# A delta-rule layer with a ternary feed-forward: weights of the output projection and the first o and A fetched in the recurrence's last cycle

## What is computed

```python
        def _delta_rule(q, k, v, a, beta):
...
            def step(St, inp):
                q_t, k_t, v_t, a_t, b_t = inp
                err = jnp.einsum('bhvk,bhk->bhv', St, k_t) - v_t
                St = a_t[..., None] * St - (b_t[..., None] * err)[..., None] * k_t[:, :, None, :]
                o_t = jnp.einsum('bhvk,bhk->bhv', St, q_t)
                return (St, o_t)
...
        o = _delta_rule(q, k, v, a, beta)
        mu = jnp.mean(o, axis=-1, keepdims=True)
        var = jnp.mean(jnp.square(o - mu), axis=-1, keepdims=True)
        o = (o - mu) * lax.rsqrt(var + 1e-05) * ln_w + ln_b
        g = jax.nn.sigmoid(x @ Wg).reshape(b, s, NH, DV)
        o = (o * g).reshape(b, s, NH * DV)
        return o @ Wo
...
        up = jnp.einsum('bsd,ed->bse', x, wu)
        gate = jnp.einsum('bsd,ed->bse', x, wg)
        hidden = jax.nn.silu(up) * gate
        return jnp.einsum('bse,de->bsd', hidden, wd)
...
    x = _layernorm(x + _L0_attn_ref(x, ...), axis=-1)
    x = _layernorm(x + _L0_ffn_ref(x, L0_ffn_W_up, L0_ffn_W_gate, L0_ffn_W_down), axis=-1)
```

## Time and profile before

| | us |
|---|---|
| median of 3 runs | 2807.29 (2800.23 to 2809.53) |
| the profiled execution | 2809.65 |
| its span, first to last instruction | 2807.9 |
| TensorE busy in it | 2580.0 |
| VectorE, GpSimd, ScalarE busy | 2031.4, 1435.8, 1204.8 |
| mean granted TensorE clock | 0.964 |

### The profile page before, as it was taken

How to read it: one execution, slowest core, us unless ns; L and a number is a source line. 1 busy time by engine, 2 the same in 40 slices (tenths; PEclk the granted TensorE clock), 3 DMA queues, 4 the chain that set the end, 5 groups by cost and what they waited for, 6 DMA issues and landing times. The chain is left out here.

```text
span 2807.9 us, 50612 instructions
## 1 busy us (share of the span) xinstructions
PE 2580.0 (92%) x17812; PEld 2217.5 (79%) x17922; DVE 2031.4 (72%) x5887; ACT 1204.8 (43%) x2393; POOL 1435.8 (51%) x1215
## 2 busy tenths in 40 slices
PE   8999999999999499999999999999639997899999
PEld 6888878887888388888888888888527776788887
DVE  4776777677768279899999999999548885433333
ACT  4455445545544233333333333334458774433333
POOL 2644543454355488999899898888222220000000
PEclk9999999999999799999999999999659998999999
DMA  5466455645654855555656665556364553100000
GB/s 132 128 176 190 143 146 168 180 142 153 174 166 123 281 187 211 197 197 207 226 225 228 223 232 208 196 206 227 123 262 164 198 206 108 80 12 11 11 11 15
DMA packets 417320, 454.39 MB, mean 162 GB/s; under 512 B 122496, under 2 KB 367232, under 8 KB 393856
## 3 DMA queue, kind: packets, MB, share of 16 engines
q1 hardware_dynamic: 417152, 452.22, 48.5%
HBM read 321.49 MB, written 131.14 MB: 161 GB/s over the span
## 5 line engine op out<-in xcount | busy, mean ns | idle before, releaser
L355 PE MATMUL pa_ps<-pa_x_hi,pa_w_hi 128*128 128x512 f32 x1296 | 507.3, 391 | 11.0 <-ACT pa_y L298 6.8
L355 PE MATMUL pa_ps<-pa_x_lo,pa_w_hi 128*128 128x512 f32 x1296 | 505.1, 390 | 0.0
L355 PE MATMUL pa_ps<-pa_x_hi,pa_w_lo 128*128 128x512 f32 x1296 | 504.9, 390 | 0.0
L438 DVE SCALAR_TENSOR_TENSOR pa_cv<-pa_y,pa_taps,pa_cv 128x2048 f32<-128x2048 f32 x144 | 354.6, 2462 | 17.8
L1182 DVE TENSOR_TENSOR pb_tmp<-pb_gb,pb_ps 128x112 f32<-128x112 f32 (+6 forms) x1792 | 331.0, 224 | 23.2 <-POOL pb_gb L774 9.3
L774 POOL TENSOR_TENSOR pb_gb<-pb_gb,pb_ng 128x448 f32<-128x448 f32 (+6 forms) x448 | 331.7, 787 | 4.2 <-DMA pb_gb<-scratch_pairs 4.2
L1187 DVE TENSOR_TENSOR pb_ps<-pb_ps,pb_tmp 128x112 f32<-128x112 f32 (+6 forms) x1792 | 332.6, 228 | 0.0
L355 PEld LDWEIGHTS pa_ps<-pa_x_hi,pa_w_hi 128*128 128x128 f32 x1296 | 243.5, 188 | 69.2 <-ACT pa_y L298 11.5
L758 POOL TENSOR_TENSOR pb_UT<-pb_UT,pb_crow 128x1024 f32<-128x1024 f32 x120 | 281.9, 2368 | 5.8 <-DMA pb_crow<-scratch_crow 5.8
L355 PEld LDWEIGHTS pa_ps<-pa_x_hi,pa_w_lo 128*128 128x128 f32 x1296 | 243.7, 188 | 51.1
L355 PEld LDWEIGHTS pa_ps<-pa_x_lo,pa_w_hi 128*128 128x128 f32 x1296 | 243.7, 188 | 50.0
(11 more groups left out here) (193 smaller groups left out, 5421.5 us busy)
## 6 DMA issues: line engine op xcount, KB each, us to landing
pb_crow<-scratch_crow SPq DMA_DIRECT2D x30, 2048.0 KB, 9.6
pb_gb<-scratch_pairs SPq DMA_DIRECT2D x64, 896.0 KB, 6.6
pa_o_ng<-scratch_beta SPq DMA_DIRECT2D x16, 1024.0 KB, 7.9
scratch_ng<-pa_o_ng SPq DMA_DIRECT2D x16, 1024.0 KB, 4.5
scratch_A<-pa_o_A SPq DMA_DIRECT2D x16, 1024.0 KB, 4.5
scratch_vt<-pa_o_vt SPq DMA_DIRECT2D x16, 1024.0 KB, 4.5
scratch_q<-pa_o_q SPq DMA_DIRECT2D x16, 1024.0 KB, 6.9
scratch_g<-pa_o_g SPq DMA_DIRECT2D x16, 1024.0 KB, 8.1
```

The costliest lines, as they stand in the source:

```text
L355: last = nc.tensor.matmul(out, w[:, mat, k, :], xx[:, k, b * S:(b + 1) * S], start=(k == 0 and n == 0), stop=(k == KT - 1 and n == 2))
L438: nc.vector.scalar_tensor_tensor(out=out, in0=yy[:, :, k:k + S], scalar=tap(k), in1=out, op0=ALU.mult, op1=ALU.add).then_inc(s_tap, 1)
```

## The change

- `res`, the tile for the stage's results (32 KB of a partition), and a pair of tiles `first` for o and A now exist during the recurrence. UT lies in `res`, KT in `first[0]`, vt in `first[1]`.
- In the recurrence's last cycle SyncE loads, when their readers are done, o of chunk 0 into KT's place, Wo into UT's, and A of chunk 0 into vt's. Behind its last step of that stage GpSimd multiplies the two. SyncE's final wait has the weights' four loads in it.
- `attention_out` finds the product of chunk 0 and the weights in place. Its buffers for A and g are its own, and SyncE starts with o and A of chunk 1.
- ScalarE and VectorE wait at their heads for nothing of the columns; the first affine step does.
- The 16 splits of the weights go in three groups of 8, 4 and 4 between the steps of chunk 0, and `low` of chunk 0 stands ahead of the normalisation of chunk 1.

```diff
-        vt = m.sb("vt", [P, HB, CH])
+        vt = first[1][:, :, :].rearrange("p g (i t) -> p (g i) t", t=CH)
...
-        KTr = m.sb("KT", [P, GR, P])
+        KTr = first[0]
...
-        UT = m.sb("UT", [P, HB, P])
+        UT = res[:, :, :].rearrange("p c (g v) -> p (c g) v", v=P)
...
                 if kind == LAST:
-                    feed_forward_weights(4, 8)
+                    feed_forward_weights(4, 6)
+                    sp.wait_ge(s_dp, at_d + D_STATE[3] + 4)
+                    sp.wait_ge(s_os[0], 16)
+                    load(first[0][:, :, :], "o", 0, s_early[0])
+                    feed_forward_weights(6, 8)
+                    sp.wait_ge(s_dp, at_d + D_S[7] + 1)
+                    for j in range(4):
+                        sp.dma_start(res[:, 4 * j:4 * j + 4, :], wo.rearrange("(h p) d -> p h d", p=P)[:, 4 * j:4 * j + 4, :]).then_inc(s_early[1], 16)
+                    feed_forward_weights(8, 9)
+                    sp.wait_ge(s_wv, 2 * c + 2)
+                    sp.wait_ge(s_w, 2 * c + 2)
+                    load(first[1][:, :, :], "A", 0, s_early[0])
                     store_o(c - 1, 1 - p, at_d)
-                    feed_forward_weights(8, PIECES)
+                    feed_forward_weights(9, PIECES)
                     return
...
+            sp.wait_ge(s_early[1], 64)
...
+            pool.wait_ge(s_early[0], 32)
+            tt(first[0][:, :, :], first[0][:, :, :], first[1][:, :, :], ALU.mult).then_inc(s_early[0], 1)
...
-            load(o_in[0], "o", 0, s_o[0])
-            load(a_in[0], "A", 0, s_a[0])
+            load(o_in[1], "o", 1, s_o[1])
+            load(a_in[1], "A", 1, s_a[1])
             sp.dma_start(lnw[:, :], ln_w.rearrange("(p o) -> p o", o=1)).then_inc(s_c, 16)
             sp.dma_start(lnb[:, :], ln_b.rearrange("(p o) -> p o", o=1)).then_inc(s_c, 16)
-            for j in range(4):
-                sp.dma_start(wo_in[j], wo.rearrange("(h p) d -> p h d", p=P)[:, 4 * j:4 * j + 4, :]).then_inc(s_wl[j], 16)
-            load(o_in[1], "o", 1, s_o[1])
+            load(g_in[0], "g", 0, s_g[0])
+            load(a_in[0], "A", 2, s_a[0])
+            load(g_in[1], "g", 1, s_g[1])
+            sp.wait_ge(s_t, 4)
+            load(o_in[0], "o", 2, s_o[0])
             load_x(0, 0)
             load_x(1, 1)
-            sp.wait_ge(s_oa, 1)
-            load(a_in[0], "A", 2, s_a[0])
-            sp.wait_ge(s_t, 4)
-            load(o_in[0], "o", 2, s_o[0])
-            sp.wait_ge(s_wo, 8)
-            load(g_in[0], "g", 0, s_g[0])
-            sp.wait_ge(s_wo, 12)
-            load(a_in[1], "A", 1, s_a[1])
-            sp.wait_ge(s_wo, 16)
-            load(g_in[1], "g", 1, s_g[1])
+            sp.wait_ge(s_oa, 2)
+            load(a_in[1], "A", 3, s_a[1])
             sp.wait_ge(s_t, 8)
             load(o_in[1], "o", 3, s_o[1])
             sp.wait_ge(s_gm, 4)
             load(g_in[0], "g", 2, s_g[0])
-            sp.wait_ge(s_oa, 2)
-            load(a_in[1], "A", 3, s_a[1])
             sp.wait_ge(s_oa, 3)
             load(a_in[0], "A", 4, s_a[0])
...
-            nc.gpsimd.memset(eps[:, :], EPS).then_inc(s_c, 1)
-            for j, (sem, start) in enumerate([(s_p, 2), (s_r, 2), (s_res, 2)]):
+            nc.gpsimd.memset(eps[:, :], EPS).then_inc(s_id, 1)
+            for j, (sem, start) in enumerate([(s_p, 2), (s_r, 2), (s_res, 2), (s_oa, 1)]):
...
-            scaled(0, 0, 0)
+                pool.wait_ge(s_o[p], 16 * i + 16 * p)
+                pool.wait_ge(s_a[p], 16 * i + 16 * p)
+                nc.gpsimd.tensor_tensor(o_in[p][:, :, :], o_in[p][:, :, :], a_in[p][:, :, :], ALU.mult).then_inc(s_oa, 1)
+
             scaled(1, 0, 1)
             scaled(2, 1, 0)
             scaled(3, 1, 1)
...
-            act.wait_ge(s_c, 33)
+            act.wait_ge(s_id, 3)
...
-                if not first:
+                if first:
+                    act.wait_ge(s_c, 32)
+                else:
                     act.wait_ge(s_lo, c - 1)
...
+            def round_weights(first, end):
+                for h in range(first, end):
+                    nc.scalar.activation(wo_hi[:, h, :], res[:, h, :], ACT.Copy).then_inc(s_wh, 1)
+
+            round_weights(0, 8)
             squares(0)
             normal(0)
-            for h in range(NH):
-                if h % 4 == 0:
-                    act.wait_ge(s_wl[h // 4], 16)
-                nc.scalar.activation(wo_hi[:, h, :], wo_in[h // 4][:, h % 4, :], ACT.Copy).then_inc(s_wh, 1)
-            act.wait_ge(s_wo, NH)
+            round_weights(8, 12)
             affine(0, 0, True)
+            round_weights(12, NH)
+            high(0, 0)
             squares(1)
             normal(1)
-            high(0, 0)
             affine(1, 1, True)
...
-            dve.wait_ge(s_c, 33)
...
+            def rest_of_weights(first, end):
+                for h in range(first, end):
+                    dve.wait_ge(s_wh, h + 1)
+                    nc.vector.tensor_tensor(wo_lo[:, h, :], res[:, h, :], fp32(wo_hi[:, h, :]), ALU.subtract).then_inc(s_wo, 1)
+
             means(0)
+            rest_of_weights(0, 8)
             normal(0, True)
-            for h in range(NH):
-                dve.wait_ge(s_wh, h + 1)
-                nc.vector.tensor_tensor(wo_lo[:, h, :], wo_in[h // 4][:, h % 4, :], fp32(wo_hi[:, h, :]), ALU.subtract).then_inc(s_wo, 1)
+            rest_of_weights(8, 12)
+            gate(0, 0, 0)
+            rest_of_weights(12, NH)
             means(1)
-            gate(0, 0, 0)
+            low(0, 0)
             normal(1)
-            low(0, 0)
...
-        recurrence(nc, scr, [W_up, W_gate, W_down], part)
         res = m.sb("res", [P, NCH, HID])
         stat = m.sb("stat", [P, NCH, 2])
-        attention_out(nc, x, Wo, ln_w, ln_b, scr, res, stat)
+        with ExitStack() as inner:
+            first = [Mem(nc, inner, "first").sb(n, [P, NH, CT]) for n in ("o", "A")]
+            recurrence(nc, scr, [W_up, W_gate, W_down], Wo, part, res, first)
+            attention_out(nc, x, ln_w, ln_b, scr, res, stat, first[0])
```

22 lines of the change are left out of this document (7 added, 15 removed).

## The result

The changed kernel takes 2788.86 us (median of 6 runs, 2784.39 to 2792.46), the kernel before beside it 2807.08 (2800.23 to 2813.46). The ratio is 0.9934, with a 95% interval of 0.9916 to 0.9951: 18.5 us less, from 13.8 to 23.6. The forecast was 2790.1 in a range of 2782 to 2798, so the time, the sign and the size came as foretold. The profiled execution of after has a span of 2790.7 us, where that of before has 2807.9.

The account below looks back on a forecast made before the run. The output projection's first product, at 2101.02, sets the rest. Minus 11.1 (start), minus 8.4 (splits), plus 2.0 and 1.3 (VectorE), minus 1.1 (og_lo) gives about 17.2 us earlier: 2790.1 us, range 2782 to 2798.

Parts of the forecast that it names:

- Start of the block: Head of the output projection: TensorE starts at about 2035.9, 11.1 us earlier; eight weight splits ahead of the squares are free.
- First stall: VectorE, chunk 0: GpSimd's multiplication for chunk 1 stops the weight subtractions; reciprocal at 2049.7 instead of 2047.7, 2.0 us lost.
- Second stall: VectorE, before chunk 1's sums: GpSimd's multiplication for chunk 2 holds the last of four subtractions from 2055.5 to 2060.0.
- then the sums: 2068.1: VectorE, chunk 1: after one subtraction, the gate and four more subtractions, the sums end at 2068.1; squares start at 2068.2.
- Squares to first product: From chunk 1's squares to the first product: the old path in its old order, 15.6 us, from 2068.2 to 2083.8.
- Product 0: First product of the output projection: starts at 2083.8, 17.2 us before 2101.02.
- Rival E: First products on TensorE: granted 1.2 GHz; 128 more matmuls at the low clock make it 0.3% slower, about 2817; chance 0.03.
- The recurrence: Its last cycle: the added loads put piece 8 at about 1992, 2.5 us before ScalarE reads it, cost zero.
- rival C: Recurrence's last cycle: early loads come late, piece 8 behind four weight loads; up to 6 us, gain about 10, 2797; chance 0.11.
- B: VectorE's short instructions keep their turn beside GpSimd: 2.0 and 3.9 us not lost, gain 23, about 2784; chance 0.20.
- D: Loop behind the first product isn't ready: up to 5 us of the gain lost in the first chunks, 2795; chance 0.10.
- F: Block's start doesn't move, because the barrier waits for a load or a multiplication: within 0.3%, 2806; chance 0.04.

Follow-up runs that it names:

- all splits first: The changed kernel with all 16 weight splits between normalisation and affine step of chunk 0, and 16 subtractions ahead of the gate; ratio 0.9952 to the kernel before.
- early weights alone: The changed kernel, but o and A of chunk 0 loaded and multiplied in the projection as before, only Wo early; ratio 0.9971 to the kernel before.
- the columns at the heads: The changed kernel with the layer norm's columns awaited at the heads of ScalarE and VectorE again; ratio 0.9964 to the kernel before.
- GpSimd held back: The changed kernel with three added waits that start GpSimd's multiplications for chunks 1, 2 and 3 later; ratio 0.9918 to the kernel before.

## Why the prediction was right, point by point

- **Start of the block: right.** 0.97 us from the block's first load (1.0 in the sum), 11.1 us gained. The eight splits ahead of the squares are free: the squares start at 5.67 us (5.5), and ScalarE even waits 0.67 us for VectorE in front of them.
- **First stall: right.** The eight subtractions took 9.21 us, the reciprocal is at 14.68 us (14.8). The affine step is at 20.00 (20.2), 17.7 us ahead of before (17.5).
- **Second stall: right.** GpSimd's multiplication for chunk 2 starts at 20.29 us (20.6) and holds the subtractions for 4.3 us. The one that was held is the last of the four ahead of the gate, as I had it (5.02 us for 0.68). With these multiplications held back, that time comes back, and with one more it grows.
- **The step that failed: "then the sums: 2068.1".** I knew that the fourth multiplication (chunk 3's) would come at about 31 us, and asked only whether it would hold og_lo. It held pc_nmu, 0.17 us long, which stands in front of the squares: 2.8 us. The fault was in my reading of what can be held ("the same kind as the weight subtractions, both inputs in SBUF"). The trace of before had the row against it. VectorE's groups from 2035 to 2366 us there show a copy with one input of 128x6 elements, 12 times at 2968 ns and 4 times at 162:

```profile
L1561 DVE COPY pc_bn_all<-pc_bn 128x6 f32 x12 | 35.6, 2968 | 0.0
...
L1561 DVE COPY pc_bn_all<-pc_bn 128x6 f32<-128x6 f32 x4 | 0.7, 162 | 0.0
```

  One of them starts at 2123.51 and ends with GpSimd's multiplication, 2121.93 plus 4.61. The same gap made the expectation miss for the kernel with all splits first, and half of it for early weights alone. The other half there, and the kernel with the columns at the heads, is pc_shift: it has both inputs in SBUF, so my reading covered it, but at 0.17 us I hadn't priced it.
- **Squares to first product: sized a little too long.** 15.6 us in the sum, 14.5 in the trace. Part of it is TensorE: the twelve transposes of chunk 2 took 2.47 us, and 2.82 before.
- **Product 0: its clock was left out of the sum.** I kept its length. It took 1.6 us less, because the clock was already at the higher level: it was granted 1.00 from 2087.0 to 2098.0 us, and 0.52 from 2101.0 to 2104.2 before. Its matmuls follow one another by 0.23 us once the second has begun, where the first seven took 0.44 each. Rival E had the clock on the other side.
- So product 1 is at 50.25 us where 48.9 was foretold: 2.5 late for the squares, 1.1 back behind them; and the 1.6 of product 0 makes the total right, 17.5 for 17.2. That the total hit so well is luck in part: one error of 2.5 us, and two of 1.1 and 1.6 the other way.
- **The recurrence: cost zero, but with less margin than I gave it.** The load of Wo is at 1979.99; ScalarE reads piece 8 at 1996.50, 40.4 us ahead of the block's start as before (1994.51, 40.4 ahead), and its row names no idle time. But the piece, issued at 1982.60, took 13.6 us to land, until 1996.2: 0.3 us early, not 2.5. And ScalarE does wait for the next one, piece 9:

```profile
1996.50 0.61 ACT L859 ACTIVATE pb_kq<-pb_kq 128x512 f32<-128x512 f32 x1
...
2004.75 0.63 ACT L859 ACTIVATE pb_kq<-pb_kq 128x512 f32<-128x512 f32 x1 [2.68 <-DMA pb_kq<-in_W_down]
```

  That wait is in every profile of a kernel in which o, Wo and A all come early (0.3 to 3.4 us) and in none of the others. It costs nothing, because ScalarE's next copy of X, at 2010.53, waits 3.84 us for VectorE: it is 26.4 us ahead of the block's start in both kernels (2008.50 before). Piece 8 was the closer one: the copy of X behind it, at 1998.08, waits 0.26 us for VectorE, so by an estimate from these rows some 0.6 us more (0.3 and 0.26) would have begun to cost time, as in rival C.

  Over all profiles, the block starts between 2027.3 and 2038.9 us. The twelve profiles of kernels with early loads have a mean of 2032.4, the two without 2034.9 and 2029.9, mean 2032.4 as well. This spread, up to 0.4% of the time, is there in kernels that are the same up to this point. It is larger than most effects of this study, and of the size of the scatter that gives a 17 us gain an interval of 10 us. Where it comes from stays open.
- **The rivals.** B (no stalls): refuted; held back by hand, the stalls' end gives 7.0 us. C (late pieces: one is, and the slack takes it), D (loop not ready; the transposes at 2098.20 name no idle time), E (lower clock through the first products) and F (start doesn't move) are refuted by the rows above.

## What to carry to other kernels

When an early stage is moved forward, the chain that was second becomes the one to price: here VectorE between GpSimd's multiplications, where 17.7 us won at the affine step left 15.9 at the first product. Before adding or moving work of GpSimd, list every VectorE instruction beside it, the shortest too, and look in the trace for instructions whose duration is many times their least: a 0.17 us instruction that someone waits for costs as much as a large one. Where GpSimd has slack, a wait that puts it behind VectorE's step is free; three waits of that kind gave 7.0 us here by the traces, and the order of the sums, with a different place for one of the waits, 2.4 more.

## What the runs showed of the hardware

VectorE and GpSimd stand still for each other, whole instructions long and in both directions. Held until the end of GpSimd's multiplication were instructions with two inputs in SBUF, large and small (weight subtractions, gate, og_lo, and pc_shift on 128x16: 2.67 and 3.28 us for 0.17) and, unexpected, one-input ones: pc_nmu (TENSOR_SCALAR, 128x16: 2.42, 2.49, 2.99 and 4.26 us for 0.17) and the copy on 128x6 (about 3.0 us for 0.16, 12 of 16 in every profile). Not held were instructions that read PSUM (eight of pc_nrm in 2.63 us at 2045.61, with GpSimd at work from 2045.77, in the kernel with GpSimd held back), the RECIPROCAL on 128x16 in SBUF (0.25 us at 2054.60 with early weights alone and at 2060.04 with the columns at the heads, in the middle of a multiplication), and BATCH_NORM_STATS2 on 128x512 in SBUF (0.69 to 0.70 us in each of the 12 chunks of a profile in which it starts beside GpSimd). So neither the size nor the number of inputs alone tells which instruction is held. The other way round, GpSimd took 6.47 us for 4.5 when og_lo, 2.28 us long, had started 0.17 us earlier. In a row of short instructions VectorE doesn't keep its turn: beside subtractions and gate GpSimd took 4.56 to 5.02 us for 4.49, so it was in after at most 0.5 us, and then held the next of them to its end.

The Trainium skill's page "SBUF — State Buffer", section "SBUF: two separate sides", states an exclusive lock, held by whichever starts first for its whole length, between a GpSimd instruction and a VectorE instruction that has two SBUF inputs or runs in a 2-port performance mode. The runs agree for both directions (3.28 us for 0.17 on VectorE, 6.47 for 4.5 on GpSimd) and for the two-input ones. The one-input cases would fall under its second half; no trace shows in which mode an instruction ran, so that this is why pc_nmu and the copy are held and RECIPROCAL isn't stays an argument.
